# Second attention of a two-layer decoder: the order of the 48 small score products of a unit

## The chip, the cores and the metric

The kernel runs on one core of one Trainium2 chip. The metric is the device time of one execution in microseconds (us). The engines are TensorE (PE in the profile, with its weight loads shown apart as PEld), VectorE (DVE), ScalarE (ACT), GpSimd (POOL), and SyncE (SP), which issues most of the DMAs. Each engine works through its own list of instructions in the written order and is held by semaphores.

## The reference

Six sublayers work on `x` of 32 x 64 x 512 float32, that is 2048 tokens of 512 features. The change touches the second one, a cross attention of 32 sequences of 64 tokens onto 64 context tokens each, with 32 heads that share 8 key groups (4 heads to a group, 16 features to a head):

```python
def _L0_xattn_ref(q, k, v, start_pos, mask):
    N_HEADS = 32
    N_KV_HEADS = 8
    N_REP = N_HEADS // N_KV_HEADS
    HEAD_DIM = 512 // N_HEADS
    xq = q.reshape(b, s, N_KV_HEADS, N_REP, HEAD_DIM)
    xk = k.reshape(b, t, N_KV_HEADS, HEAD_DIM)
    xv = v.reshape(b, t, N_KV_HEADS, HEAD_DIM)
    scores = jnp.einsum('bsgrd,btgd->bgrst', xq, xk) / math.sqrt(HEAD_DIM)
    scores = scores + mask
    probs = jax.nn.softmax(scores.astype(jnp.float32), axis=-1).astype(q.dtype)
    out = jnp.einsum('bgrst,btgd->bsgrd', probs, xv)
    return out.reshape(b, s, N_HEADS * HEAD_DIM)
...
    x = x + _L0_attn_ref(_layernorm(x, axis=-1), ...)
    x = x + _L0_xattn_ref(_layernorm(x, axis=-1), ctx_1024, ctx_1024, 0, mask_SxS2_ff0)
    x = x + _L0_ffn_ref(_layernorm(x, axis=-1), ...)
```

## The kernel before

The program keeps all of `x` in SBUF as 16 tiles of 128 tokens (`held.X`, two sequences to a tile) and goes through the six sublayers one after the other. `part_b` is the second attention. It works in 32 units: unit n takes token tile t = n // 2 and one half of its heads, 16 heads, in PSUM slot n % 2. The units whose number is even also bring in the next token tile, so even and odd units differ.

To be near float32, a product of two operands is three products of fp16 numbers: high by high, high by low and low by high, which is what the helper `mm3` (lines 116 to 118) issues. Three different places of the program go through these three lines; in the trace the names tell them apart. `p_up<-wd_lo,d_xt_high` with 32\*64 and 32x128 are the score products (`scores`, the call at lines 1533 to 1535), `p_y<-wd_lo,wf_hi` with 128\*64 and 128x34 are the products of probabilities and values (`attend`, call at line 1565).

The scores of a unit are four pieces of work for TensorE, all into the two PSUM banks `banks` of its slot: two products that lay down the mask (line 1520), two that add its small part (line 1525, 64 rows each), then 48 small ones, in three nested loops: over the bank r (two), the feature block k (four) and the sequence s (two), with the three products of `mm3` innermost. Bank r reads the partitions 32 r to 32 r + 31, so it sits in its own strip of 32 rows of the array; sequence s writes the PSUM partitions 64 s to 64 s + 63, so it sits in its own half of the columns. Every one of the 48 is 32 rows by 64 columns and takes 128 columns of moving data. Two banks by two sequences are four tiles of the array that have nothing in common.

The order of one iteration n, engine by engine, is written out:

- TensorE: `turn_p(n)` transposes the probabilities (line 1555, 8 transposes; waits for the exponentials), `shift(n+1)` subtracts the row maximum (line 1543; waits for `peak`), `scores(n+2)`, in even units `turn`, the transposes of the next token tile (line 110), and `attend(n-1)`. `attend` waits last for `z_ready`, which `norm_o(n-2)` counts up.
- VectorE: `low_p(n)` (line 246, two pieces), `norm_o(n-2)` (lines 1382 and 1385), in odd units `add` (1393), `peak(n+2)` (line 1370, the row maximum, waits for the scores), and in even units `low_x` (1361) and `measure` (1399 and 1401).
- ScalarE: `high_p(n)` (line 1472, two pieces; waits for `turn_p`), `expo(n+1)` (1463), and the work on the next tile: `norm` (1431), `high_x` (1439; waits for `turn`), `high_keys` (1449), `keys` (1454).
- GpSimd: the low parts of keys and values of coming tiles (1309, 1318, 1324, 1329).

After the last unit the next sublayer, `part_c`, follows in the same lists; four of its steps are already woven into the last units.

Of the kernel before, what the change touches and what calls it, by code (L numbers as in the profile page):

```python
# [28 lines left out]
KB = D // 128  # L29
# [77 lines left out]
def transpose_tile(nc, held, ps, xn):  # L107

    for k in range(KB):
        last = nc.tensor.transpose(ps[:, 128 * k:128 * k + 128], xn[:, 128 * k:128 * k + 128], held.ident[:])  # L110
    return last


def mm3(nc, ps, st, mv, start, stop):

    nc.tensor.matmul(ps, st[0], mv[0], start=start, stop=False)  # L116
    nc.tensor.matmul(ps, st[0], mv[1], start=False, stop=False)  # L117
    return nc.tensor.matmul(ps, st[1], mv[0], start=False, stop=stop)  # L118
# [1108 lines left out]
def part_b(nc, held, a, es):  # L1227

    p = Part()
    if True:  # L1230
# [8 lines left out]
        xn, xt = held.d_xn, held.d_xt  # L1239
        kt, bd, ks, cd, vb = held.b_kt, held.b_bd, held.b_ks, held.b_cd, held.b_vb  # L1240
# [5 lines left out]
        p_s, p_t, p_x, p_v = held.p_up, held.p_y[:, 0:2, :], held.p_y[:, 2, :], held.p_y[:, 3, :]  # L1246
# [18 lines left out]
        if True:  # L1265
# [236 lines left out]
            def tensor(pe):  # L1502
                pe.sem_inc(v_ready, VW)

                def turn(t):
                    pe.wait_ge(xn_ready, t + 1)
                    if t:
                        pe.wait_ge(xt_ready, t)
                    transpose_tile(nc, held, p_x, xn[:, t % 2, :]).then_inc(tr_ready, 1)

                def scores(n):

                    slot, t = n % 2, n // 2
                    pe.wait_ge(xt_ready, t + 1)
                    pe.wait_ge(bd_ready, 2 * t + 5)
                    if n >= 2:
                        pe.wait_ge(exp_ready, n - 1)
                    banks = (2 * slot, 2 * slot + 1)
                    for r in banks:
                        nc.tensor.matmul(p_s[:, r, :], held.onehot[:],  # L1520
                                         held.mk01[:].rearrange("p (a k) -> p a k", a=1).broadcast_to([128, 8, S]),
                                         start=True, stop=False)
                    for q, r in enumerate(banks):
                        half = slice(64 * q, 64 * q + 64)
                        nc.tensor.matmul(p_s[:, r, :], held.onehot[half, :],  # L1525
                                         held.mk2[half, :].rearrange("p (a k) -> p a k", a=1).broadcast_to([64, 8, S]),
                                         start=False, stop=False)
                    for r in banks:
                        pair = slice(32 * r, 32 * r + 32)
                        for k in range(KB):  # L1530
                            for s in range(2):
                                seq = slice(128 * (t % TC) + 64 * s, 128 * (t % TC) + 64 * s + 64)
                                last = mm3(nc, p_s[64 * s:64 * s + 64, r, 128 * k:128 * k + 128],
                                           [x[pair, k, seq] for x in xt], [x[pair, :, k, seq] for x in bd],
                                           False, k == KB - 1)
                    last.then_inc(s_ready, 1)

                def shift(n):

                    slot = n % 2  # L1540
                    pe.wait_ge(top_ready, n + 1)
                    for q in range(2):
                        last = nc.tensor.matmul(p_s[:, 2 * slot + q, :], held.ident16[:],  # L1543
                                                top[:, slot, 8 * q:8 * q + 8].rearrange("p (h a) -> p h a", a=1)
                                                .broadcast_to([128, 8, S]), start=False, stop=True,
                                                skip_group_check=True)
                    last.then_inc(sub_ready, 1)

                def turn_p(n):
                    pe.wait_ge(exp_ready, n + 1)  # L1550
                    for q in range(2):
                        if n:
                            pe.wait_ge(pt_ready, 2 * n + q - 1)
                        for k in range(KB):
                            last = nc.tensor.transpose(p_t[:, q, 128 * k:128 * k + 128],  # L1555
                                                       prob[:, n % 2, 8 * q + 2 * k:8 * q + 2 * k + 2, :]
                                                       .rearrange("p h k -> p (h k)"), held.ident[:])
                        last.then_inc(t_ready, 1)

                def attend(n):  # L1560
                    slot, t = n % 2, n // 2
                    pe.wait_ge(pt_ready, 2 * n + 2)
                    pe.wait_ge(vb_ready, VB * t + 3 * VB)
                    if n:
                        pe.wait_ge(z_ready, n)
                    for k in range(KB):
                        for q in range(2):
                            for s in range(2):
                                at = VC * (2 * k + q)
                                last = mm3(nc, p_v[64 * s:64 * s + 64, at:at + VC],  # L1570
                                           [w[:, slot, q, 128 * k + 64 * s:128 * k + 64 * s + 64] for w in pt],
                                           [w[:, 2 * (t % TC) + s, 2 * k + slot, :, :].rearrange("p h n -> p (h n)")
                                            for w in vb], True, True)
                    last.then_inc(v_ready, 1)
                def keep_warm(times):
                    for _ in range(times):
                        nc.tensor.matmul(p_v, held.ident16[:],
                                         held.ident16[:].rearrange("p (a n) -> p a n", a=1).broadcast_to([128, 4, 128]),
                                         start=True, stop=True)

                keep_warm(8)
                turn(0)
                keep_warm(5)
                turn(1)
                for n in range(-2, N + 1):
                    if 0 <= n < N:
                        turn_p(n)
                    if n == -1:
                        keep_warm(5)
                    if 0 <= n + 1 < N:  # L1590
                        shift(n + 1)
                    if n + 2 < N:
                        scores(n + 2)
                    if n >= 0 and n % 2 == 0 and n // 2 + 2 < NT:
                        turn(n // 2 + 2)
                    if n == N - 2:
                        p.c.trans(pe, 0)
                        p.c.trans(pe, 1)
                    if n == N - 1:
                        p.c.aux(pe, 0)  # L1600
                        p.c.main(pe, 0)
                    if n >= 1:
                        attend(n - 1)
# [1381 lines left out]
```

## Time and profile before

| | |
|---|---|
| device time, median of 3 runs | 1169.84 us (1168.39 to 1173.36) |
| the profiled execution | 1173.24 us |
| its span in the trace | 1171.5 us |
| the second attention in it | about 206 to 352 us |
| TensorE busy over the span | 1107.2 us, 95% |
| VectorE busy over the span | 673.3 us, 57% |

The span is the time from the first to the last instruction in the trace; the profiled execution is 1.74 us longer than its span, and 3.40 us longer than the median of the three runs. Small products overlap each other in the array, so a row of them counts each one's full duration from its start to its modelled end: what two neighbouring rows are apart in their starts is what the work costs, not the duration of one.

### The profile page before, as it was taken

How to read it: one execution, taken by the hardware profiler on the slowest of the kernel's cores; microseconds unless marked ns; L12 is line 12 of the kernel's file. 1: busy time of each engine (PE TensorE's matmuls, PEld its weight loads, DVE VectorE, ACT ScalarE, POOL GpSimd, SP SyncE). 2: the span in 40 equal slices, each digit the busy share in tenths (PEclk: the TensorE clock that was granted, in tenths of full speed). 3: DMA queues.
4: the chain of work that ended last, by engine and by line, in shares of the span. 5: the costliest groups of instructions: out<-in, count | busy, mean ns of one | idle time of the engine just before them, and what ended most of it. 6: DMA issues, size and time to landing. Idle time of an engine off the chain costs nothing.

```text
span 1171.5 us, 24189 instructions
## 1 busy us (share of the span) xinstructions
PE 1107.2 (95%) x9595; PEld 585.8 (50%) x9595; DVE 673.3 (57%) x1205; ACT 502.4 (43%) x999; POOL 376.1 (32%) x339
## 2 busy tenths in 40 slices
PE   7988988999998989999999999999989899999996
PEld 3445544777774444444444444444455544444442
DVE  7688785788887774435213511531278724656465
ACT  5466773888864644322112211211279732223221
POOL 2254574666641320000380070000044400516073
PEclk9999999999998999999999999999999999999998
DMA  7000000111110211320020000000000000000000
GB/s 246 2 3 4 23 9 15 49 46 45 48 56 4 87 45 43 94 77 1 21 70 13 0 21 33 1 1 1 1 10 13 2 1 1 21 16 27 9 36 37
DMA packets 29013, 35.94 MB, mean 31 GB/s; under 512 B 5882, under 2 KB 20499, under 8 KB 28788
## 3 DMA queue, kind: packets, MB, share of 16 engines
q1 hardware_dynamic: 27506, 34.53, 9.3%
q8 instruction: 68, 1.11, 0.4%
q10 hardware_dynamic: 1410, 0.06, 0.1%
q14 instruction: 29, 0.24, 0.1%
HBM read 30.24 MB, written 4.19 MB: 29 GB/s over the span
## 4 chain that ended last, share of the span: by engine, by line
PE 75%; DVE 5%; ACT 1%; issue 1%; POOL 0%; DVEq 0%; POOLq 0%; ACTq 0%
PE p_up L116 11%; PE p_up L117 11%; PE p_up L118 11%; PE p_y L116 10%; PE p_y L118 9%; PE p_y L117 9%; PE p_y L1555 3%; PE p_up L110 2%; PE p_up L1543 1%; PE p_up L1520 1%; PE p_up L2387 1%; PE p_y L2418 1%; PE p_y L2408 1%; ACT wd_hi L2342 1%; PE p_up L1525 1%
## 5 line engine op out<-in xcount | busy, mean ns | idle before, releaser
L1982 DVE TENSOR_TENSOR d_h_low<-d_hf,d_h_high 128x512 f16<-128x512 f32 (+1 forms) x40 | 27.9, 697 | 205.1 <-ACT d_h_high L2071 205.1
L116 PE MATMUL p_up<-d_xt_high,wd_hi 128*128 128x512 f16 (+1 forms) x352 | 134.1, 381 | 2.9 <-PE p_y L118 1.5
L117 PE MATMUL p_up<-d_xt_low,wd_hi 128*128 128x512 f16 (+1 forms) x352 | 134.2, 381 | 0.0
L118 PE MATMUL p_up<-d_xt_high,wd_lo 128*128 128x512 f16 (+1 forms) x352 | 134.0, 381 | 0.0
L170 ACT ACTIVATE d_sg<-p_up 128x512 f32<-128x512 f32 (+1 forms) x40 | 23.8, 594 | 212.8 <-PE p_up L118 212.7
L116 PE MATMUL p_y<-wd_hi,d_h_high 128*128 128x512 f16 (+1 forms) x272 | 103.1, 379 | 0.0
L118 PE MATMUL p_y<-wd_hi,d_h_low 128*128 128x512 f16 (+1 forms) x272 | 103.1, 379 | 0.0
L117 PE MATMUL p_y<-wd_lo,d_h_high 128*128 128x512 f16 (+1 forms) x272 | 103.1, 379 | 0.0
L437 POOL TENSOR_TENSOR a_pt_low<-a_ex,a_pt_high 128x1024 f16<-128x1024 f32 x32 | 68.1, 2128 | 76.6 <-ACT a_pt_high L926 76.5
L138 POOL TENSOR_SCALAR wd_raw<-wd_raw 128x1156 f32<-128x1156 f32 x8 | 25.1, 3140 | 208.8 <-DVE d_h_low L1982 208.8
L2252 POOL TENSOR_TENSOR wd_hi<-wd_hi,e_den 128x1024 f32<-128x1024 f32 x16 | 30.6, 1909 | 133.3 <-DVE e_den L2288 133.3
L2582 DVE TENSOR_TENSOR d_h_low<-d_hf,d_h_high 128x512 f16<-128x512 f32 x32 | 28.6, 893 | 66.1 <-ACT d_h_high L2680 66.1
L116 PE MATMUL p_up<-d_xt_high,wf_hi 128*128 128x512 f16 x160 | 60.9, 381 | 0.0
L117 PE MATMUL p_up<-d_xt_low,wf_hi 128*128 128x512 f16 x160 | 60.9, 381 | 0.0
L118 PE MATMUL p_up<-d_xt_high,wf_lo 128*128 128x512 f16 x160 | 60.9, 380 | 0.0
L116 PEld LDWEIGHTS p_up<-d_xt_high,wd_hi 128*128 128x128 f16 (+1 forms) x352 | 35.4, 101 | 45.3 <-issue 3.8
L2673 ACT ACTIVATE d_sg<-p_up 128x512 f32<-128x512 f32 x32 | 19.1, 596 | 88.9 <-PE p_up L118 88.9
L118 PEld LDWEIGHTS p_up<-d_xt_high,wd_lo 128*128 128x128 f16 (+1 forms) x352 | 35.4, 101 | 41.1 <-issue 0.8
L117 PEld LDWEIGHTS p_up<-d_xt_low,wd_hi 128*128 128x128 f16 (+1 forms) x352 | 35.4, 100 | 40.4 <-issue 0.7
L1309 POOL TENSOR_TENSOR wd_lo<-wd_lo 128x512 f16<-128x512 f32 x30 | 34.7, 1158 | 44.4 <-ACT wd_lo L1454 39.9
L116 PE MATMUL p_y<-wf_hi,d_h_high 128*128 128x512 f16 x128 | 48.5, 379 | 0.1
L117 PE MATMUL p_y<-wf_lo,d_h_high 128*128 128x512 f16 x128 | 48.5, 379 | 0.0
(342 smaller groups left out, 2890.7 us busy)
## 6 DMA issues: line engine op xcount, KB each, us to landing
wd_raw<-in_w_d SPq DMA_DIRECT2D x16, 616.0 KB, 3.7
wd_raw<-in_w_f SPq DMA_DIRECT2D x8, 578.0 KB, 3.8
X<-in_x SPq DMA_DIRECT2D x4, 1024.0 KB, 12.1
wd_lo<-in_ctx_t SPq DMA_DIRECT2D x128, 32.0 KB
out_x<-wd_raw SPq DMA_DIRECT2D x16, 256.0 KB, 2.0
wd_lo<-in_ctx SPq DMA_DIRECT2D x32, 64.0 KB, 2.3
wd_raw<-in_w_c SPq DMA_DIRECT2D x1, 1096.0 KB, 12.4
wd_hi<-in_Wo SPq DMA_DIRECT2D x1, 1024.0 KB
```

The costliest lines, as they stand in the source:

```text
L110: last = nc.tensor.transpose(ps[:, 128 * k:128 * k + 128], xn[:, 128 * k:128 * k + 128], held.ident[:])
L116: nc.tensor.matmul(ps, st[0], mv[0], start=start, stop=False)
L117: nc.tensor.matmul(ps, st[0], mv[1], start=False, stop=False)
L118: return nc.tensor.matmul(ps, st[1], mv[0], start=False, stop=stop)
L138: nc.gpsimd.tensor_scalar(raw, raw, WS, None, ALU.mult).then_inc(done, 1)
L170: nc.scalar.activation(sg[0:n, (j + G6) % 2, :], p_up[0:n, 2 * (j % 2), :], ACT.Silu, scale=1.0 / (XS * WS)).then_inc(sg_ready, 1)
L437: nc.gpsimd.tensor_tensor(pt[1][:, n % 3, :, :], ex[:, n % 2, :, :], pt[0][:, n % 3, :, :], ALU.subtract).then_inc(pt_ready, 1)
L1309: nc.gpsimd.tensor_tensor(bd[1][:, h, :, 128 * i:128 * i + 128], ks.rearrange("p (k n) -> p k n", k=KB), bd[0][:, h, :, 128 * i:128 * i + ...
L1555: last = nc.tensor.transpose(p_t[:, q, 128 * k:128 * k + 128], prob[:, n % 2, 8 * q + 2 * k:8 * q + 2 * k + 2, :] .rearrange("p h k -> p ( ...
L1982: nc.vector.tensor_tensor(hid[1][0:n, d % NH, :], value, hid[0][0:n, d % NH, :], ALU.subtract).then_inc(h_ready, 1)
L2252: nc.gpsimd.tensor_tensor(prob[:, t % 3, :, :], prob[:, t % 3, :, :], den[:, t % 2, :].rearrange("p (j a) -> p j a", a=1).broadcast_to([12 ...
L2582: nc.vector.tensor_tensor(hid[1][:, f % NH, :], sq[:, f % 2, :], hid[0][:, f % NH, :], ALU.subtract).then_inc(h_ready, 1)
```

## The change

`scores` issues the same 48 products with the same operands into the same places, and only their order differs. The loops are now feature block, term of the three, sequence, bank, with the bank innermost, so that four successive products go to the four tiles and a tile's next product comes four later. `mm3` is no longer called here, so the trace will give them another line (1534). The last product carries the semaphore as before. The other engines' lists are untouched.

```diff
-                    for r in banks:
-                        pair = slice(32 * r, 32 * r + 32)
-                        for k in range(KB):
+                    for k in range(KB):
+                        for term, (x, w) in enumerate(((xt[0], bd[0]), (xt[0], bd[1]), (xt[1], bd[0]))):
                             for s in range(2):
                                 seq = slice(128 * (t % TC) + 64 * s, 128 * (t % TC) + 64 * s + 64)
-                                last = mm3(nc, p_s[64 * s:64 * s + 64, r, 128 * k:128 * k + 128],
-                                           [x[pair, k, seq] for x in xt], [x[pair, :, k, seq] for x in bd],
-                                           False, k == KB - 1)
+                                for r in banks:
+                                    pair = slice(32 * r, 32 * r + 32)
+                                    last = nc.tensor.matmul(p_s[64 * s:64 * s + 64, r, 128 * k:128 * k + 128],
+                                                            x[pair, k, seq], w[pair, :, k, seq],
+                                                            start=False, stop=k == KB - 1 and term == 2)
                     last.then_inc(s_ready, 1)
```

In TensorE's list the first unit's scores stood like this before. Here `mk` and `onehot` are the mask products, `d_xt_high` and `d_xt_low` the two fp16 parts of the tokens, `wd_lo` the buffer in which the keys lie; six of the sixteen triples are shown.

```order
1023 L1520 MATMUL p_up<-mk,onehot 128x512 x2
1024 L1525 MATMUL p_up<-mk,onehot 128x512 x2
1025 L116 MATMUL p_up<-wd_lo,d_xt_high 64x128
1026 L117 MATMUL p_up<-wd_lo,d_xt_high 64x128
1027 L118 MATMUL p_up<-wd_lo,d_xt_low 64x128
1028 L116 MATMUL p_up<-wd_lo,d_xt_high 64x128
1029 L117 MATMUL p_up<-wd_lo,d_xt_high 64x128
1030 L118 MATMUL p_up<-wd_lo,d_xt_low 64x128
```

Each triple is one tile of the array, and the first 24 products all belong to the first bank. In the changed kernel the same place of the list reads:

```order
1023 L1520 MATMUL p_up<-mk,onehot 128x512 x2
1024 L1525 MATMUL p_up<-mk,onehot 128x512 x2
1025 L1534 MATMUL p_up<-wd_lo,d_xt_high 64x128 x8
1026 L1534 MATMUL p_up<-wd_lo,d_xt_low 64x128 x4
1027 L1534 MATMUL p_up<-wd_lo,d_xt_high 64x128 x8
1028 L1534 MATMUL p_up<-wd_lo,d_xt_low 64x128 x4
1029 L1534 MATMUL p_up<-wd_lo,d_xt_high 64x128 x8
1030 L1534 MATMUL p_up<-wd_lo,d_xt_low 64x128 x4
1031 L1534 MATMUL p_up<-wd_lo,d_xt_high 64x128 x8
1032 L1534 MATMUL p_up<-wd_lo,d_xt_low 64x128 x4
```

A feature block is now 12 products, 8 with the high part of the tokens (two terms by four tiles) and 4 with the low part. What stands before and behind the 48 did not move.

## Rows read from the trace of the kernel before

**Rows 1.** The page: busy time by engine over the span.
```profile
PE 1107.2 (95%) x9595; PEld 585.8 (50%) x9595; DVE 673.3 (57%) x1205; ACT 502.4 (43%) x999; POOL 376.1 (32%) x339
```
**Rows 2.** Busy time by stretches of the second attention.
```profile
core 0: us, PE busy (x) PEld busy (x) DVE busy (x) ACT busy (x) POOL busy (x), PEclk, DMA share, GB/s
215.00:326.00 111.00, 111.00 (x2654) 83.94 (x2649) 97.85 (x165) 93.09 (x145) 71.85 (x93) 1.00 0.20 57
326.00:333.00 7.00, 6.29 (x119) 4.40 (x113) 4.14 (x7) 4.44 (x7) 3.67 (x5) 0.76 0.16 43
```
**Rows 3.** Timeline of TensorE, odd unit: start us, us, engine, line, operation.
```profile
257.63 1.09 PE L1555 MATMUL p_y<-ident,wf_hi 128*128 128x128 f32 x8
258.56 0.59 PE L1543 MATMUL p_up<-b_top,ident 128*128 128x512 bf16 x2
...
259.52 0.39 PE L1525 MATMUL p_up<-mk,onehot 64*128 64x512 bf16 x2
259.84 0.25 PE L116 MATMUL p_up<-wd_lo,d_xt_high 32*64 32x128 f16 x2
259.92 0.22 PE L117 MATMUL p_up<-wd_lo,d_xt_high 32*64 32x128 f16 x2
259.98 0.22 PE L118 MATMUL p_up<-wd_lo,d_xt_low 32*64 32x128 f16 x2
...
260.33 0.26 PE L116 MATMUL p_up<-wd_lo,d_xt_high 32*64 32x128 f16 x4
260.41 0.24 PE L117 MATMUL p_up<-wd_lo,d_xt_high 32*64 32x128 f16 x4
260.46 0.24 PE L118 MATMUL p_up<-wd_lo,d_xt_low 32*64 32x128 f16 x4
260.52 0.22 PE L116 MATMUL p_up<-wd_lo,d_xt_high 32*64 32x128 f16 x2
...
260.97 0.22 PE L118 MATMUL p_up<-wd_lo,d_xt_low 32*64 32x128 f16 x2
261.12 0.21 PE L116 MATMUL p_y<-wd_lo,wf_hi 128*64 128x34 f16 x2
...
261.87 0.19 PE L118 MATMUL p_y<-wd_lo,wf_lo 128*64 128x34 f16 x2
```
**Rows 4.** Timeline of TensorE, the even unit behind it.
```profile
261.99 1.09 PE L1555 MATMUL p_y<-ident,wf_hi 128*128 128x128 f32 x8
262.95 0.61 PE L1543 MATMUL p_up<-b_top,ident 128*128 128x512 bf16 x2
...
265.36 0.22 PE L118 MATMUL p_up<-wd_lo,d_xt_low 32*64 32x128 f16 x2
265.52 0.66 PE L110 MATMUL p_y<-ident,d_xn 128*128 128x128 f32 x4
266.10 0.21 PE L116 MATMUL p_y<-wd_lo,wf_hi 128*64 128x34 f16 x2
...
266.98 1.09 PE L1555 MATMUL p_y<-ident,wf_hi 128*128 128x128 f32 x8
```
**Rows 5.** Timeline of VectorE over the same two units.
```profile
257.49 0.69 DVE L1361 SCALAR_TENSOR_TENSOR d_xt_low<-p_y,d_xt_high 128x512 f16<-128x512 f32 x1
...
259.01 1.29 DVE L246 SCALAR_TENSOR_TENSOR wf_lo<-p_y,wf_hi 128x512 f16<-128x512 f32 x2
...
260.50 0.42 DVE L1385 TENSOR_TENSOR wf_lo<-p_y,b_rec 128x256 f32<-128x256 f32 x1
...
261.68 1.21 DVE L1370 TENSOR_REDUCE b_top<-p_up 128x16 bf16<-128x1024 f32 x1
263.38 1.29 DVE L246 SCALAR_TENSOR_TENSOR wf_lo<-p_y,wf_hi 128x512 f16<-128x512 f32 x2 [0.49 <-ACT wf_hi L1472]
...
264.87 0.42 DVE L1385 TENSOR_TENSOR wf_lo<-p_y,b_rec 128x256 f32<-128x256 f32 x1
265.64 1.23 DVE L1370 TENSOR_REDUCE b_top<-p_up 128x16 bf16<-128x1024 f32 x1 [0.35 <-PE p_up L118]
266.84 0.69 DVE L1361 SCALAR_TENSOR_TENSOR d_xt_low<-p_y,d_xt_high 128x512 f16<-128x512 f32 x1
```
**Rows 6.** The first units: what unit 0 waits for.
```profile
205.48 1.01 ACT L1463 ACTIVATE wf_hi<-p_up 128x1024 f32<-128x1024 f32 x1
206.54 1.09 PE L1555 MATMUL p_y<-ident,wf_hi 128*128 128x128 f32 x8
206.63 1.23 DVE L1370 TENSOR_REDUCE b_top<-p_up 128x16 bf16<-128x1024 f32 x1 [2.75 <-PE p_up L118]
207.91 0.61 PE L1543 MATMUL p_up<-b_top,ident 128*128 128x512 bf16 x2 [0.28 <-DVE b_top L1370]
```
**Rows 7.** Timeline of TensorE: the first transpose of units 3 and 26.
```profile
220.27 0.44 PE L1555 MATMUL p_y<-ident,wf_hi 128*128 128x128 f32 x2
...
328.27 1.93 PE L1555 MATMUL p_y<-ident,wf_hi 128*128 128x128 f32 x8
334.90 0.55 PE L1555 MATMUL p_y<-ident,wf_hi 128*128 128x128 f32 x3
```
**Rows 8.** The chain that ended last, at the stop of TensorE: start us, us, what.
```profile
327.37 0.71 issue
```

## The prediction

> **What bounds the kernel now.** I read the page's busy table first. TensorE is busy 95% of the span and VectorE 57% [rows 1], but that is an average over six sublayers, so the next view is busy time by stretches, for the second attention alone. Between 215 and 326 us TensorE shows no idle time at all, while VectorE is busy 97.85 of 111 us, ScalarE 93.09 and GpSimd 71.85 [rows 2]. TensorE sets the pace there, but VectorE stands close behind at 88%, so a faster TensorE will soon wait. How much is in it must be read from the timelines of one pair of units.
>
> An odd unit runs on TensorE from 257.63 to 261.99, 4.36 us [rows 3, 4]; the even unit behind it from 261.99 to 266.98, 4.99 us [rows 4]. The pair is 9.35 us, and it repeats: 11.4 such pairs fit between unit 3 at 220.27 and the stop at 327 us, told below. Unless said otherwise, times below are counted from the unit's first transpose.
>
> **What the 48 products cost now.** The first starts at 259.84 and the last pair at 260.97: 1.13 us [rows 3]. The rows show why. Two products stand in each row, one for each sequence, and rows are 0.055 to 0.06 us apart: both column halves work side by side, and within a tile a product follows the one before it after about 0.056 us. The first bank is alone from 259.84 to 260.33, 0.49 us; then rows of four appear, 260.33 to 260.46, where both banks run; then the second bank is alone to the end. So the four tiles can run together, and do for some three steps, and their step does not grow there: 260.33, 260.41, 260.46, 260.52 is 0.055 to 0.06 again once the second bank has had its longer first step (0.08).
>
> **What the new order makes of it.** Each tile has 12 products in a chain. With all four started at once the last pair starts after one first step of 0.08 and ten of 0.056, 0.64 us, plus 0.02 for the three tiles that start behind the first: 0.66. I take 0.66, so the block is 0.47 us shorter (1.13 - 0.66). Bounds: if issue of the 96 instructions (a load and a product each) limits, the nearest row is the value products, where 48 go from 261.12 to 261.87, 24 pairs at 0.033 us [rows 3]; the block would then be 24 x 0.033 = 0.79, and 0.34 is saved. The other end is 0.49, the whole time in which the first bank was alone. The step of four tiles is shown by few rows, which is why I keep 0.34 to 0.49.
>
> **Odd units: next to nothing.** `attend` begins at 261.12, right behind the last score product [rows 3]. But it also waits for `norm_o`, whose second operation ends at 260.50 + 0.42 = 260.92 [rows 5]. From VectorE's end to TensorE's start a wait costs at least 0.05 (206.63 + 1.23 = 207.86, and line 1543 starts at 207.91 [rows 6]). So with the scores done 0.47 earlier `attend` can start at 260.97 to 261.05 at best, and the unit gains 0.07 to 0.15, not 0.47. What is late next is therefore a chain that begins at the unit's own first transpose and holds no score product: transposes, `high_p`, `low_p`, `norm_o`, `attend`, 3.29 us from the transpose to the end of `norm_o`, whatever TensorE does between. I take 0.08 for it.
>
> **Even units: most of it.** The transposes of the next tile stand between scores and `attend`, so `attend` begins at 266.10, 4.11 after the first transpose [rows 4], while `norm_o` ended at 265.29, after 3.30 [rows 5]: 0.7 us of room, and the 0.47 goes through. Two things take some back:
>
> - `shift` waits for `peak` of the unit before. `peak` ran 261.68 to 262.89 and `shift` began at 262.95 [rows 4, 5], already on its heels. `peak` there is fixed by VectorE's list from the odd unit's transposes on. If the odd unit shortens by 0.08, `shift` comes 0.08 later within the even unit; if it does not, because VectorE is late (next point), `peak` is late by as much. Either way `shift` is about 0.08 later. The even unit saves 0.47 - 0.08 = 0.39 and lasts 4.60.
> - VectorE's list in the even unit: `norm_o` ends at 3.30, `peak` can start at 3.33 (the scores are there at about 3.2), now 3.65 [rows 5]. From `peak` to `low_x` is 1.20, from `low_x` to the next `low_p` 1.52 (257.49 to 259.01) [rows 5]: 3.33 + 1.20 + 1.52 = 6.05. The next unit starts at 4.60, so its `low_p` starts 1.45 after its transposes instead of 1.38 (259.01 - 257.63). That 0.07 goes down the chain to `attend` and eats the odd unit's 0.08.
>
> So an odd unit stays at 4.35, an even one becomes 4.60, a pair 8.95, and the saving is 0.40 of a possible 0.94. VectorE's busy time in a pair is 97.85 / 111 x 9.35 = 8.24 us, so it would be 92% busy.
>
> **How many.** Twelve even units, 4 to 26, bring in a tile: 12 x 0.39 = 4.7 us. Odd units and unit 28, which has no tile, with 0.02 each: 0.3. The first units are different: unit 0 waits for the exponentials (205.48 + 1.01 = 206.49, start 206.54 [rows 6]), behind ScalarE's own list, so the savings of the first two blocks vanish there; but `shift` in unit 0 waited for a `peak` that began at 206.63 [rows 6] and will begin up to 0.94 earlier, and units 0 to 2 hold little VectorE work. From unit 0 to unit 3 it is 13.73 us [rows 6, 7]; three blocks of 0.47 and the wait of about 0.4 would be 1.8. I take 1.3, between 0.5 and 1.8. Sum: 4.7 + 0.3 + 1.3 = 6.3 us. From the profiled execution that is 1173.24 - 6.3 = 1166.9.
>
> That execution lies 3.40 above the median. Part of it is visible: TensorE stops for 0.71 us before unit 26 [rows 8], and the granted clock of 326 to 333 us is 0.76 [rows 2]; unit 26 takes 334.90 - 328.27 = 6.63 us [rows 7], 1.64 over its like. I do not count on that stop coming or going and take the sum from the median: 1169.84 - 6.3 = 1163.5. What follows the second attention waits for its end, in the same lists, so the saving carries through; no DMA, buffer or other engine's list is moved.
>
> **Rivals.**
>
> 1. *The tiles do not get closer.* If TensorE could not start small products closer than now, 1.13 / 46 = 0.025 us apart on average, nothing would change: 1169.8. Against it: value products start 0.0163 us apart (0.033 for two), and while both banks run four start in 0.056 [rows 3]. The Trainium skill, "TensorE: Matmul & The Clock Gate", section "Wait — 56ns, not 53.3ns?", says that start-to-start never falls below about 25 ns however small the product; as an estimate from it, the 48 would need 1.2 us and this rival would hold. By that rule, the trace disagrees: 0.0163. Chance 0.08.
>
> 2. *All of it arrives.* If the waits I found moved along (the chain over `high_p` and `norm_o` ran faster because fewer accesses collide), 30 blocks of 0.47 would give 14.1 us, 1155.7. Against it: that chain's 3.29 and 3.30 us are the same in an odd and an even unit, though TensorE does other work in them. Chance 0.06.
>
> 3. *The first part of VectorE's and GpSimd's chain binds harder.* If keys or maxima fall behind, an even unit gains only 0.15 to 0.2 and the sum is 2.5 to 3: 1167. For it: VectorE at 88% of a stretch; against it: 8.95 - 8.24 leaves 0.7 us in a pair. Chance 0.17.
>
> 4. *Slower, by the clock.* TensorE will hold about 6% of idle time in this stage (0.94 - 0.40 of 8.95). After the stop at 327 us the granted clock fell and unit 26 cost 1.64 us more [rows 2, 7]. If the new gaps, up to 0.2 us each but in every unit, let it fall again and again, each fall costs some 1.6: four cancel the gain, eight make it 1163.5 + 13 = 1176.7. Against it: the stop was one stretch of 0.71 us in which nothing ran [rows 8], and the clock stood at 1.00 over 111 us with `shift` already waiting in even units. Chance 0.06. A change of tile at each product that made the four take turns, 48 x 0.056 = 2.7 us a block, would add 50 us; the rows of four speak against it, 0.01.
>
> The forecast has the remaining 0.62.
>
> **How the numbers follow.** A measurement of this kernel can tell about 0.5%, 5.85 us, from no change, and the limit is then 1163.99: my value is just under it. Of the forecast's 0.62 I give 0.40 to faster and 0.22 to same. With rival 2 that is 0.46 faster; rivals 1 and 3 and a light case of the clock give 0.22 + 0.08 + 0.17 + 0.01 = 0.48 same; slower 0.06. The forecast's own range is 1161 to 1166.5 (block saving 0.34 to 0.49, first units 0.5 to 1.8, and a median that moves by 1 us). To leave out no more than 2 in 10 it goes down to 1158 toward rival 2 and up to 1170.5, over rivals 3 and 1.
>
> **What would show it.** In the profile after: the score rows hold four products each and their block lasts 0.66 us; an odd unit stays at 4.3 to 4.36 us while an even one falls to 4.6; `attend` in odd units starts 0.05 to 0.12 behind the end of line 1385's operation, with a gap of some 0.3 us on TensorE before it; VectorE's wait for the scores before `peak` is gone; the clock stays at 1.00. A block over 0.8 us, an odd unit under 4.25, an even unit over 4.8, or a clock under 1.00 between 215 and 320 us would prove a step wrong.

## The result, and the profile after

| | before | changed |
|---|---|---|
| median, us | 1169.06 (1164.46 to 1173.36, 10 runs) | 1163.18 (1160.56 to 1169.35, 10 runs) |
| ratio, 95% interval | | 0.9948 (0.9927 to 0.9969) |
| profiled execution, its span | 1173.24, 1171.5 | 1160.63, 1158.9 |

The change saves 5.9 us of the medians; the interval of the ratio makes that 3.6 to 8.5 us. In a second comparison, told below, the ratio was 0.9950 (0.9935 to 0.9965; 1164.74 against 1170.59). The forecast was 1163.5.

The page's busy table, beside [rows 1]:

```profile
PE 1086.5 (94%) x9595; PEld 568.2 (49%) x9595; DVE 669.7 (58%) x1205; ACT 502.0 (43%) x999; POOL 375.4 (32%) x339
```

TensorE fell from 95 to 94% of a shorter span, which says little. The stretch of the second attention says more; columns as in [rows 2]: the stretch, its length, busy time of each engine, then TensorE's granted clock, the DMA share and GB/s.

```profile
212.00:323.00 111.00, 104.49 (x2730) 75.26 (x2734) 99.97 (x170) 96.94 (x151) 75.17 (x98) 1.00 0.21 60
```

TensorE had no idle time in 111 us before [rows 2]; now 6.5 us of 111 are idle, and VectorE is at 90% in place of 88%. The timeline of TensorE in the changed kernel shows an odd unit and the even one behind it (start us, us, engine, line, operation, idle time before it), beside [rows 3, 4]:

```profile
252.57 1.09 PE L1556 MATMUL p_y<-ident,wf_hi 128*128 128x128 f32 x8
253.50 0.59 PE L1544 MATMUL p_up<-b_top,ident 128*128 128x512 bf16 x2
...
254.78 0.30 PE L1534 MATMUL p_up<-wd_lo,d_xt_high 32*64 32x128 f16 x8
254.92 0.22 PE L1534 MATMUL p_up<-wd_lo,d_xt_low 32*64 32x128 f16 x4
254.97 0.28 PE L1534 MATMUL p_up<-wd_lo,d_xt_high 32*64 32x128 f16 x8
...
255.42 0.22 PE L1534 MATMUL p_up<-wd_lo,d_xt_low 32*64 32x128 f16 x4
256.02 0.21 PE L116 MATMUL p_y<-wd_lo,wf_hi 128*64 128x34 f16 x2 [0.37 <-DVE wf_lo L1385]
```
```profile
256.89 1.09 PE L1556 MATMUL p_y<-ident,wf_hi 128*128 128x128 f32 x8
257.88 0.60 PE L1544 MATMUL p_up<-b_top,ident 128*128 128x512 bf16 x2
...
259.17 0.30 PE L1534 MATMUL p_up<-wd_lo,d_xt_high 32*64 32x128 f16 x8
...
259.96 0.66 PE L110 MATMUL p_y<-ident,d_xn 128*128 128x128 f32 x4
260.55 0.21 PE L116 MATMUL p_y<-wd_lo,wf_hi 128*64 128x34 f16 x2
...
261.42 0.55 PE L1556 MATMUL p_y<-ident,wf_hi 128*128 128x128 f32 x3
```

The block runs from 254.78 to 255.42, 0.64 us against 1.13 [rows 3]; a feature block's 12 products take 0.17 to 0.19. The odd unit lasts 256.89 - 252.57 = 4.32 us, and its last row is the one to look at: `attend` starts 0.6 us after the last score row, after 0.37 us of idle time that `norm_o` (line 1385) ends. The even unit has no such gap before `attend` and lasts 4.53 us against 4.99 [rows 4]. VectorE over the same two units, beside [rows 5]:

```profile
253.96 1.29 DVE L246 SCALAR_TENSOR_TENSOR wf_lo<-p_y,wf_hi 128x512 f16<-128x512 f32 x2
...
255.44 0.42 DVE L1385 TENSOR_TENSOR wf_lo<-p_y,b_rec 128x256 f32<-128x256 f32 x1
...
256.62 1.21 DVE L1370 TENSOR_REDUCE b_top<-p_up 128x16 bf16<-128x1024 f32 x1
258.27 1.29 DVE L246 SCALAR_TENSOR_TENSOR wf_lo<-p_y,wf_hi 128x512 f16<-128x512 f32 x2 [0.45 <-ACT wf_hi L1472]
...
260.10 1.22 DVE L1370 TENSOR_REDUCE b_top<-p_up 128x16 bf16<-128x1024 f32 x1
```

`norm_o` ends at 255.86 and `attend` starts at 256.02, 0.16 us behind it, where the forecast had 0.05 to 0.12. The wait for the scores before the even unit's `peak` (0.35 us in [rows 5]) is gone: it starts at 260.10, 3.21 us after the first transpose.

Where the time of the whole stage went, from the starts of the units in the two traces:

| | before, us | changed, us | saved |
|---|---|---|---|
| units 0 to 2 | 13.74 | 13.58 | 0.16 |
| units 3 to 24 (11 pairs) | 102.67 | 97.68 | 4.99 |
| unit 25 (with a stop of TensorE) | 5.33 | 5.48 | -0.15 |
| unit 26 | 6.63 | 4.46 | 2.17 |
| units 27 to 30 | 16.31 | 16.16 | 0.15 |
| sum | 144.68 | 137.36 | 7.32 |

Both traces hold a stop of TensorE in unit 25 for which the chain of waits names no releaser, before as in [rows 8] and in the changed kernel as

```profile
319.28 0.93 issue
```

but only before did the granted clock fall behind it, to 0.76 over 326 to 333 us [rows 2]. That is 1.66 of the 2.17 us of unit 26 (6.63 against 4.97 for its like), so the change's own saving in this stage is about 5.7 us. What the stop is comes in the last section.

### The profile page after: what moved, and what is told of

Its sections match the earlier page's. It is cut to its first block, busy times and chain, and to the rows that moved or that the text cites. A ratio compares the mean times of both kernels' runs of the same rounds, so it can differ in the third digit from the quotient of the medians.

```text
span 1158.9 us, 24189 instructions
## 1 busy us (share of the span) xinstructions
PE 1086.5 (94%) x9595; PEld 568.2 (49%) x9595; DVE 669.7 (58%) x1205; ACT 502.0 (43%) x999; POOL 375.4 (32%) x339
## 4 chain that ended last, share of the span: by engine, by line
PE 67%; DVE 8%; ACT 3%; POOL 3%; issue 2%; POOLq 0%; DVEq 0%; ACTq 0%
PE p_up L116 10%; PE p_up L117 10%; PE p_up L118 10%; PE p_y L116 9%; PE p_y L118 9%; PE p_y L117 9%; PE p_up L110 2%; DVE wf_lo L246 2%; PE p_up L2388 1%; PE p_y L2419 1%; PE p_y L2409 1%; ACT wd_hi L2343 1%; POOL wd_lo L1309 1%; PE p_y L1556 1%; PE p_y L2416 1%
## 5 line engine op out<-in xcount | busy, mean ns | idle before, releaser
L246 DVE SCALAR_TENSOR_TENSOR wf_lo<-p_y,wf_hi 128x512 f16<-128x512 f32 x64 | 41.2, 686 | 13.6 <-ACT wf_hi L1472 13.5
L2343 ACT ACTIVATE wd_hi<-p_up,e_top 128x128 f32<-128x128 f32 x128 | 45.0, 384 | 8.1 <-DVE e_top L2283 8.1
```

The lines of the kernel that those rows point to most:

```text
L246: nc.vector.scalar_tensor_tensor(pt[1][:, slot, b, :], p_t[:, b, :], PS, pt[0][:, slot, b, :], ALU.mult, ALU.subtract).then_inc(pt_ready, 1)
L2343: last = nc.scalar.activation(prob[:, t % 3, j, :], scores[:, j, :], ACT.Exp, bias=top[:, t % 2, j:j + 1], accum_out=den[:, t % 2, j:j + 1])
```

## The experiments

Times of units are from the traces, from first transpose to first transpose; odd and even units are numbered as in the code. Where a kernel ran in one execution alone, its total is weak evidence and its units are what is read.

**The two kernels once more.** No edit.

> The changed kernel itself once more, beside the others of this call. Both theories: ratio to before 0.993 to 0.997; odd units 4.32 us, even ones 4.46 to 4.54 us. It also shows how much the trace of a second execution differs outside the second attention.

> The kernel before once more, for a second trace. Expected: odd units 4.36 us, even ones 4.98; whether TensorE stops for 0.7 us near the end of the second attention with the clock at half behind it is open, and so is how far the time outside this sublayer moves from one execution to the next.

Changed: 1164.74 us, ratio 0.9950 (0.9935 to 0.9965); odd units 4.31, even 4.46 to 4.54 us, units 0 to 30 in 137.62 us. Before: odd 4.36, even 4.98, units 0 to 30 in 144.80 us, again with a stop in unit 25 and unit 26 at 6.42 us. Inside this stage the traces repeat to 0.3 us. Outside they do not: unit 0 starts at 206.54 and 207.63 us in the two traces of before and at 203.67 and 206.50 in the two of the changed kernel, and from unit 31 to the end it is 820.3 and 816.5 us in the two of before, 817.9 and 819.2 in the two of the changed kernel. The next sublayer shows one reason, the granted clock in it (columns as above; before, then its second trace):

```profile
344.00:440.00 96.00, 84.30 (x787) 46.36 (x786) 72.01 (x202) 49.05 (x100) 23.48 (x22) 0.93 0.14 42
```
```profile
344.00:440.00 96.00, 84.13 (x853) 47.28 (x851) 73.39 (x203) 50.36 (x104) 23.58 (x23) 0.98 0.14 42
```

So a single total is worth some 4 us either way, and I read causes from the units.

**Bank outermost, terms in turn.** The edit is against the changed kernel; the lines inside the loops stay.

```diff
-                    for k in range(KB):
-                        for term, (x, w) in enumerate(((xt[0], bd[0]), (xt[0], bd[1]), (xt[1], bd[0]))):
-                            for s in range(2):
-                                for r in banks:
+                    for r in banks:
+                        for k in range(KB):
+                            for term, (x, w) in enumerate(((xt[0], bd[0]), (xt[0], bd[1]), (xt[1], bd[0]))):
+                                for s in range(2):
```

> The changed kernel with the bank as the outermost loop again and the three terms still taken in turn over the two sequences. Theory (four tiles run together only if both banks are among the next few products): the 48 products take 1.13 us again, an odd unit 4.36 us, an even one 4.98, ratio to the kernel before 1.000 (0.997 to 1.003). Rival (it is the turn among the terms that brought the gain, since a tile's next product no longer stands right behind the last one): the block stays near 0.60 us and the ratio near 0.995.

Ratio 0.999 (0.9968 to 1.0012). TensorE's timeline of this kernel, an odd unit:

```profile
259.42 0.30 PE L1534 MATMUL p_up<-wd_lo,d_xt_high 32*64 32x128 f16 x4
...
259.89 0.22 PE L1534 MATMUL p_up<-wd_lo,d_xt_low 32*64 32x128 f16 x2
259.90 0.32 PE L1534 MATMUL p_up<-wd_lo,d_xt_high 32*64 32x128 f16 x8
260.04 0.24 PE L1534 MATMUL p_up<-wd_lo,d_xt_low 32*64 32x128 f16 x4
...
260.54 0.22 PE L1534 MATMUL p_up<-wd_lo,d_xt_low 32*64 32x128 f16 x2
```

The second bank starts at 259.90, 0.48 us late, rows of double count last only for a moment, and the block is 1.12 us. Odd units 4.35, even 4.97. The turn among the terms brings nothing.

**Triples kept, bank inside.** These loops stand in place of those of the kernel before.

```diff
+                    for k in range(KB):
+                        for s in range(2):
+                            for r in banks:
+                                last = mm3(nc, p_s[64 * s:64 * s + 64, r, 128 * k:128 * k + 128], ...)
```

> The changed kernel with the three products of a tile back to back as before, but the bank inside the sequence: feature block, sequence, bank, then the triple. Theory (the array's tiles are fed apart from each other some way ahead, and only the bank's place counts): all four tiles start within 0.05 us, the block takes 0.60 to 0.70 us, an even unit 4.5 to 4.6 us, ratio to before as for the changed kernel, 0.992 to 0.998. Rival (products start strictly in their written order, so a triple holds up those behind it): in every four triples only the ends overlap, the block takes 48 x 0.056 x 2/3 = 1.8 us and the kernel is slower than before by about 0.65 x 30 = 20 us, ratio 1.017.

Ratio 0.991 (0.9881 to 0.994). TensorE's timeline, an even unit:

```profile
260.75 0.27 PE L116 MATMUL p_up<-wd_lo,d_xt_high 32*64 32x128 f16 x4
260.83 0.24 PE L117 MATMUL p_up<-wd_lo,d_xt_high 32*64 32x128 f16 x4
260.89 0.24 PE L118 MATMUL p_up<-wd_lo,d_xt_low 32*64 32x128 f16 x4
260.94 0.24 PE L116 MATMUL p_up<-wd_lo,d_xt_high 32*64 32x128 f16 x4
```

All four tiles work from the start though 9 products of three other tiles stand in the list between the first tile's triple and its next one; the block is 0.64 us, odd units 4.31, even 4.56. The whole effect of the change is the bank's place. The ratio lies a little under the expected 0.992, but the order itself is not better than that of the changed kernel: units 3 to 24 take 97.92 us against 97.68. Its trace has no stop in unit 25 (4.31 us), which is 1.2 us of its better total.

**One term of three.** The two terms with a low part are left out of the computation.

```diff
-                        for term, (x, w) in enumerate(((xt[0], bd[0]), (xt[0], bd[1]), (xt[1], bd[0]))):
+                        for term, (x, w) in enumerate(((xt[0], bd[0]),)):
...
```

> The changed kernel with only the first of the three terms of each score product, 16 products in place of 48; the two terms with a low part are left out of the computation. Theory (in odd units attend waits for norm_o, a chain from the unit's own transposes): the block falls from 0.60 to about 0.16 us, yet an odd unit stays at 4.32 us (4.29 to 4.35), and attend starts at 3.41 us after the first transpose as now; an even unit falls from 4.53 to between 4.1 and 4.4, where VectorE's or shift's wait ends it. Rival (attend in odd units still follows the scores): an odd unit falls by 0.4 to 3.9 us.

The block is 16 products, 0.19 us from its first start to its last; an odd unit lasts 4.34 us and an even one 4.32. With 32 of 48 products gone the odd unit did not shorten at all. In the even unit `attend` now waits for `norm_o` too:

```profile
265.26 0.42 PE L1534 MATMUL p_up<-wd_lo,d_xt_high 32*64 32x128 f16 x16
265.61 0.66 PE L110 MATMUL p_y<-ident,d_xn 128*128 128x128 f32 x4
266.50 0.21 PE L116 MATMUL p_y<-wd_lo,wf_hi 128*64 128x34 f16 x2 [0.23 <-DVE wf_lo L1385]
```

So 3.4 us from the first transpose to `attend` and 0.9 us for it is a floor of 4.3 us for either kind of unit, as long as `norm_o` stands behind `low_p`. The stage took 136.26 us, 1.1 less than the changed kernel's, and the total of this one execution was 1166.1. The granted clock fell twice within the stage, where the changed kernel has 1.00:

```profile
215.00:235.00 20.00, 17.45 (x332) 11.31 (x334) 15.27 (x26) 17.43 (x28) 13.36 (x17) 0.91 0.18 50
300.00:315.00 15.00, 13.56 (x253) 8.86 (x256) 13.12 (x24) 12.13 (x19) 9.62 (x13) 0.89 0.15 41
```

Each fall came behind a long wait of TensorE, one of 1.58 us for ScalarE and one of 1.21 us for GpSimd, and the unit behind it was long, 5.61 us in unit 2 (5.23 in the changed kernel) and 5.59 in unit 22 (most of its even units last 4.32):

```profile
218.43 1.63 PE L1556 MATMUL p_y<-ident,wf_hi 128*128 128x128 f32 x8 [1.58 <-ACT wf_hi L1463]
306.21 0.21 PE L116 MATMUL p_y<-wd_lo,wf_hi 128*64 128x34 f16 x2 [1.21 <-POOL wd_lo L1318]
```

**The products twice.** The scores come out doubled.

```diff
-                        for term, (x, w) in enumerate(((xt[0], bd[0]), (xt[0], bd[1]), (xt[1], bd[0]))):
+                        for term, (x, w) in enumerate(((xt[0], bd[0]), (xt[0], bd[1]), (xt[1], bd[0])) * 2):
...
```

> The changed kernel with the three terms issued twice, 96 products in place of 48, so the scores come out doubled. Theory (0.4 us of room before attend in odd units, none in even ones): the block grows by 12 x 0.056 = 0.67 us; an odd unit grows by 0.67 - 0.40 = 0.27 to about 4.6 us, an even one by 0.6 to 0.67 to about 5.15 us. Rival (no room, the products are on the path in both): both grow by 0.67 us, the odd one to 5.0.

Most odd units last 4.54 us, 0.22 more than 4.32, for 0.67 us of added products: the room is there, and 0.05 larger than I had it. The shortest even units last 5.13, 0.60 more. The others are irregular, 5.35 to 6.25 us, with gaps on TensorE that the chain puts down to issue, 0.88 us at the longest before unit 25. The last section tells what these are. Total 1180.17, one execution.

**`norm_o` ahead of `low_p`, in the changed kernel and in the one before.**

```diff
+                    if 2 <= n < N - 2:
+                        norm_o(n - 2)
                     if 0 <= n < N:
                         low_p(n)
-                    if 2 <= n < N - 2:
-                        norm_o(n - 2)
```

> The changed kernel with norm_o(n-2) ahead of low_p(n) in VectorE's list. Theory (attend waits for z_ready from norm_o, which stands behind low_p, which waits for ScalarE's high_p): norm_o now runs while VectorE waited for high_p, attend in odd units starts right behind the scores, 3.0 to 3.2 us after the first transpose, or where low_p(n-1) leaves it; an odd unit falls from 4.32 to 3.9 to 4.1 us. VectorE's own work, 97.85/111 of 9.35 us or 8.24 us in a pair plus its small gaps, keeps the pair at 8.5 or more: pair 8.85 to about 8.6, 3 us in all, ratio to before 0.990 to 0.995. Rival (the odd unit is held by something else from its transposes on, such as expo): the pair stays at 8.85 and the ratio at 0.995.

> The kernel before with norm_o(n-2) ahead of low_p(n). Theory (before the change TensorE's own work ended every unit, and norm_o was early by some 0.08 us): an odd unit stays at 4.36 us and an even one at 4.98, pair 9.34. Rival (norm_o already held attend in odd units): an odd unit falls under 4.3 us.

On the changed kernel the ratio to before is 0.9897 (0.9876 to 0.9918), 1158.02 us. TensorE, an odd unit's end and the next unit:

```profile
259.16 0.22 PE L1534 MATMUL p_up<-wd_lo,d_xt_low 32*64 32x128 f16 x4
259.31 0.21 PE L116 MATMUL p_y<-wd_lo,wf_hi 128*64 128x34 f16 x2
...
260.19 1.09 PE L1556 MATMUL p_y<-ident,wf_hi 128*128 128x128 f32 x8
261.27 0.60 PE L1544 MATMUL p_up<-b_top,ident 128*128 128x512 bf16 x2
...
264.81 1.09 PE L1556 MATMUL p_y<-ident,wf_hi 128*128 128x128 f32 x8
```

`attend` follows the scores by 0.15 us as it did before the change, and an odd unit is 3.88 us, 0.44 less: the part of the saving that the chain had kept. The even unit grew from 4.53 to 4.62, since `shift` starts 1.08 us after its transposes in place of 0.99: it waits for `peak`, which ends at 261.22. A pair is 8.50, a little under the expected 8.6, save for units 14 and 22, which last 5.03. The ratio fell just under its expected range too; this trace has no stop in unit 25 (3.98 us), which is worth 1.1 us, and whether `norm_o`'s place has a part in that no run shows. On the kernel before, the same edit leaves odd units at 4.36 and even ones at 4.95 (4.98): nothing held `attend` there, and 0.03 is `shift`'s small wait. One execution, 1167.62.

**GpSimd's variance steps between the halves of a key tile.** `rstd_next(c - 2)` moves into the key loop of `tile`, before its second half. The edit also lifts a wait out of all but the last two calls, so what it gives is that of both together.

```diff
                     for h in range(2):
+                        if h == 1 and i == 1 and c >= 2:
+                            rstd_next(c - 2)
...
-                    pool.wait_ge(vb_ready, VB * (min(TC * c + 2 * TC, NT) + 2))
+                    if c >= NC - 2:
+                        pool.wait_ge(vb_ready, VB * (min(TC * c + 2 * TC, NT) + 2))
...
-                    rstd_next(c - 1)
+                rstd_next(NC - 2)
                 rstd_next(NC - 1)
```

> The changed kernel with GpSimd's four variance steps of a chunk of tiles moved from between two key tiles to between the two halves of one, where GpSimd waits about 1 us for ScalarE. Theory (these steps make the keys of a tile late, ScalarE's keys waits for them with high_p queued behind it): the two odd units of 4.59 us, one in eight, fall to 4.32 us; 0.5 us in all. Rival (they are held by something else at the chunk's border): they stay at 4.59.

From unit 3 on all odd units but unit 25 last 4.32 us; the changed kernel has 4.59 in units 13 and 21, where `rstd_next` stands in front of a key tile. The even units behind them rise from 4.46 to 4.53, so units 3 to 24 gain 0.39 us and not 0.5. One execution, 1162.21.

**`keys(2,1)` later.**

```diff
                     if 0 <= n + 1 < N:
                         expo(n + 1)
+                    if n == 1:
+                        keys(2, 1)
...
-                    if n % 2 == 0 and n // 2 + 2 < NT:
+                    if n % 2 == 0 and n // 2 + 2 < NT and n != 0:
                         keys(n // 2 + 2, 1)
```

> The changed kernel with ScalarE's keys(2,1) moved behind high_p(1) and expo(2). Theory (in the first units ScalarE waits for GpSimd's keys with the probabilities of unit 1 queued behind): units 0 to 2, 13.58 us from the first transpose of unit 0 to that of unit 3, fall by 1.5 to 2 us. Rival (GpSimd's own row of tiles 1 and 2 sets the pace, so the wait only moves to unit 2 or 3): they fall by less than 0.5 us.

Units 0 to 2 fell from 13.58 to 12.44 us, but unit 3 rose from 4.32 to 5.21. Here is why, ScalarE and GpSimd of this kernel in unit 3:

```profile
220.36 0.72 ACT L1454 ACTIVATE wd_lo<-wd_lo,mask_bs 128x512 f32<-128x512 f32 x1 [1.42 <-POOL wd_lo L1309]
220.99 1.06 ACT L1472 ACTIVATE wf_hi<-p_y 128x512 f16<-128x512 f32 x2
```
```profile
217.38 1.41 POOL L1329 TENSOR_TENSOR wd_lo<-wd_lo 64x256 f16<-64x256 f32 x2
219.16 1.16 POOL L1309 TENSOR_TENSOR wd_lo<-wd_lo 128x512 f16<-128x512 f32 x1 [0.37 <-POOL wd_lo L1329]
```

ScalarE waits for GpSimd's keys (line 1309, behind the values of the tile before, 1329) with `high_p` (1472) queued behind. The wait only moved by two units; up to unit 4 the saving is 0.25 us. The rival had the mechanism right, the wait that moves to unit 3; its number for units 0 to 2, under 0.5 us, was not met (1.14), nor was the theory's 1.5 to 2. One execution, 1162.79.

**All three, and the first two of them.**

> The changed kernel with three changes: norm_o ahead of low_p; GpSimd's variance steps for a chunk put between the two halves of a key tile, where it waits for ScalarE; ScalarE's keys(2,1) behind high_p and expo of unit 1. Theory: the three savings lie at different places and add up, 3 us for the pairs, 0.5 us for two odd units that lasted 0.27 longer, 1.5 to 2 us in units 0 to 2: 5 us below the changed kernel, ratio to before 0.988 to 0.992. Rival (VectorE's list is already full, and the first units are held by the keys themselves): under 1 us below the changed kernel, ratio 0.994.

> The changed kernel with norm_o ahead of low_p and GpSimd's variance steps between the two halves of a key tile, but with ScalarE's keys(2,1) in its old place. Theory (moving keys(2,1) only moved the wait from unit 1 to unit 3 or 4): from the first transpose of unit 0 to that of unit 5 it is 21.3 us, not more than with the move (21.5); pairs of 8.50 us without the long even units; ratio to before 0.986 to 0.990, the same as for all three. Rival (the move was worth 1 us or more by itself): 22.3 us or more for units 0 to 4.

All three: 0.9875 (0.9854 to 0.9896), 1154.7 us. `norm_o` and the variance steps alone: 0.9878 (0.9859 to 0.9897), 1156.06 us, and from unit 0 to unit 5 21.31 us against 21.48 with the `keys` move. Both kernels beat the changed one: their intervals end at 0.9896 and 0.9897, and its interval begins at 0.9927. The `keys` move adds nothing. By the units, `norm_o`'s place takes units 3 to 24 from 97.68 to 94.14 us and GpSimd's steps to 93.34; the totals do not tell these two apart (0.9897 with `norm_o` alone). All three came to 10 us below the changed kernel of the same comparison, where 5 were expected; 1.2 us of it is the stop in unit 25, which neither kernel's trace has (3.87 us there). TensorE is busy without a gap again, with VectorE at 93% (the second of the two kernels):

```profile
215.00:315.00 100.00, 100.00 (x2632) 71.27 (x2633) 93.00 (x165) 91.75 (x144) 70.78 (x92) 1.00 0.21 59
```

## Why the prediction was right, step by step

- **The block.** Forecast 0.66 us, measured 0.64; the step of 0.056 us holds with four tiles at work. The bound from the value products (0.79) did not bite. The two orders above show the cause: the bank's place alone decides.
- **Odd units.** Forecast: `attend` waits for `norm_o`, the unit stays at 4.35. Measured 4.32, with the wait named in the row. Shown three ways: with a third of the products left nothing is gained, twice as many cost 0.22 in place of 0.67, and `norm_o` moved forward frees 0.44.
- **Even units.** Forecast 4.60, measured 4.53 (4.46 behind a long odd one). Mis-sized by 0.07: the block gives 0.49 in place of 0.47, and `shift` comes 0.03 later in the unit (0.99 against 0.96 after the first transpose), not 0.08. `peak` of the odd unit starts 4.05 after that unit's first transpose in both kernels, as forecast, but the odd unit shortened by 0.04 only. The give-back that I had in the odd unit vanished as well: I had the even unit's `peak` starting at 3.33, behind the end of `norm_o`, and it starts at 3.21, since the two operations overlap in the profile (`norm_o` 259.76 to 260.19, `peak` from 260.10). VectorE is done with an even unit 5.90 after its first transpose (248.04 to 253.94), not 6.05, just in time for `low_p` of the next unit at 253.96. A pair saves 0.49, not 0.40 us, the two with a long odd unit about 0.25, and 11 pairs 4.99 in place of 4.5.
- **The first units.** Forecast 1.3 us, measured 0.16. This step failed. I saw `shift`'s wait for `peak` in unit 0 and counted on it; it did go, and unit 0 fell from 4.43 to 3.50, but unit 1 rose from 4.35 to 4.86 and unit 2 from 4.95 to 5.23. What decides there is ScalarE's `keys`, which waits for GpSimd with `high_p` queued behind. ScalarE in unit 1 of the changed kernel:

```profile
209.36 0.72 ACT L1454 ACTIVATE wd_lo<-wd_lo,mask_bs 128x512 f32<-128x512 f32 x1 [1.40 <-POOL wd_lo L1309]
209.99 1.07 ACT L1472 ACTIVATE wf_hi<-p_y 128x512 f16<-128x512 f32 x2
```

  The unit began at 207.16, and `high_p`, which elsewhere starts 0.76 us later, starts after 2.83; before the change it was 1.92. GpSimd's list did not move: counted from its first key operation (203.31 before, 200.44 changed) the next four of line 1309 start at 2.54, 7.75, 9.94 and 15.15 us before and at 2.54, 7.73, 9.91 and 15.12 after. The experiment with `keys` shows the same wait coming back two units later.
- **The sum.** 6.3 forecast, 5.7 in this stage by the traces without the fallen clock, 5.9 by the medians. The errors partly cancelled: 1.1 us too much in the first units, 0.5 too little in the pairs. That the answer came within 0.3 us is largely luck: one median moves by more, and that of the kernel before came out at 1169.06 where the sum started from 1169.84. The traces also hold 1.66 us of clock in unit 26 that both executions of before and the bank-outermost one have (6.63, 6.42, 6.49) and the changed kernel's two do not. The length of the stop does not decide it: the clock fell behind stops of 0.71, 0.97 and 0.81 us and stayed at 1.00 behind 0.93 and 1.21 in the changed kernel and behind 0.77 in the fourth trace with the old block, `norm_o` first (unit 26: 4.95). Whether the change keeps the clock up or two executions happened to do so is open.
- **Rivals.** "Not closer" is refuted by the block. "All of it arrives" is refuted by the odd units. "Slower, by the clock" did not come in the changed kernel, where the stage stays at 1.00 with gaps of 0.37 us in its odd units. With one term the clock did fall, behind two waits of over 1.2 us and not behind the small gaps, and the stage was 1.1 us shorter even so. The rival of a chain that binds harder was wrong for the pairs and right for the first units, though on ScalarE and GpSimd, not on VectorE.

## What to carry to other kernels

When small products go to separate tiles of the array, look in the timeline at how many share a row of starts: what counts is whether the products that come next in the list reach all the tiles, not the exact turn (all four within 12 products was enough here, 24 products for one bank first was not, and nothing between was tried). Before pricing a faster block, find for each kind of iteration the wait that ends next, and measure its distance from the present start: here 0.1 us in one kind and 0.7 in the other, from one look at two timelines. For the start of a stage, follow every engine's list and not only those two that hand each other work in the steady state. Where an engine stops and the chain names no releaser, look at when its own instructions arrived.

## What the runs showed of the hardware

- Four tiles of 32 rows by 64 columns ran at the pace of one: 48 products of 128 columns in 0.64 us, 0.056 us per step and 0.013 us per product, with two banks of PSUM written at the same time.
- The array's tiles are fed out of the written order within limits, though TensorE works through one list. With triples and the bank inside, the tenth product of the list starts in the same row as the first (260.75) and the second one behind it (260.83). With all 24 products of one bank first, the second bank began 0.48 us late, when 18 of the 24 had started; with 9 products of other tiles in between there was no delay.
- The granted clock fell behind long waits. With 32 of 48 score products left out it fell to a mean of 0.91 and 0.89 in two stretches, behind waits of 1.58 and 1.21 us, and to 0.50, the lower of its two levels (1.2 GHz), from 220 to 222 and from 308 to 310 us; it stayed at 1.00 through the changed kernel's many gaps of 0.37 us, and behind its own stops of 0.93 and 1.21 us in unit 25. So the length of a stop alone does not decide in these traces.
- TensorE's stops without a releaser are waits for its own instructions. One falls in unit 25 of seven traces (0.71 and 0.97 us before, 0.93 and 1.21 in the changed kernel, 0.81, 0.77 and 1.52 in three variants; unit 25 is within 0.2 us of its like in the other seven). The page of each kernel counts DMA packets of 16 KB in a queue for instructions (packets, MB, share; before, one term, doubled):

```profile
q8 instruction: 68, 1.11, 0.4%
q8 instruction: 60, 0.98, 0.4%
q8 instruction: 80, 1.31, 0.5%
```

TensorE's list (weight loads, products and its few other records) is 2048 records shorter with one term than before and 3072 longer with the doubled products, so these 8 packets fewer and 12 more are one packet per 256 of TensorE's instructions. From 205 to 1100 us the fourteen traces hold thirteen stops of TensorE with over 0.6 us between two starts and no releaser, seven in unit 25 and six more in the doubled kernel. Counted along that list, each stands before a number that leaves 193 when divided by 256, and each ended 1.29 to 1.54 us after the end of one of these packets. In unit 25 that packet began 2.7 to 3.3 us after the unit's first transpose in the traces with a stop and 0.4 to 2.0 us after it in those without. Why it came late is open. The stop falls in the time in which the next sublayers' weights arrive (before, 317 to 327 us):

```profile
317.00:327.00 10.00, 10.00 (x265) 7.63 (x262) 9.01 (x16) 8.40 (x14) 6.27 (x9) 1.00 0.59 188
```

A DMA share of 0.59 there, against 0.20 in the stretch as a whole [rows 2]. But the same stretch has a share of 0.53 to 0.57 in the seven traces without a stop, so this load alone does not tell them apart, and the doubled kernel has six of its stops elsewhere.
